# Row vectors by transfer, weights on GpSimd, and shared copies in a four-layer graph attention kernel on one Trainium2 core

## The reference

```python
# layer 0: 4 heads of 32
scores = where(adj == 0, -inf, q @ k.T / sqrt(32));  out = softmax(scores) @ v;  out @ wo.T + bo
# layer 1 (one head), layer 2 (8 heads of 16, plus beta*log(adj + 1e-6)), layer 3 (two GATs with MLPs between)
e = leaky_relu(s1[:, None] + s2[None, :], 0.2);  attention = softmax(masked e);  out = attention @ h
# layer 3: relu(x W + b) -> GAT over all pairs, 256 wide -> elu(elu) + residual -> relu(x W + b)
#          -> GAT over adj, 128 wide -> elu(elu) + residual -> relu
```

## Time and profile before

| | us |
|---|---|
| median of 3 runs | 1078.31 |
| lowest, highest | 1078.24, 1078.61 |
| the profiled execution | 1080.22 |
| its span, first to last instruction | 1078.4 |

### The profile page before, as it was taken

One profiled execution on the slowest core, in us unless ns is written; L12 is line 12 of the kernel. 1 busy time (PEld: TensorE's weight loads), 2 busy tenths in 40 slices (PEclk: granted clock), 3 DMA queues, 4 the chain that ended last, 5 costly groups with the idle time before them and its releaser, 6 DMA issues. The chain is left out here.

```text
span 1078.4 us, 26660 instructions
## 1 busy us (share of the span) xinstructions
PE 1024.1 (95%) x9189; PEld 760.1 (70%) x9189; DVE 914.3 (85%) x2533; ACT 771.2 (72%) x2029; POOL 272.7 (25%) x606
## 2 busy tenths in 40 slices
PE   7989999999999999999999999999999999899985
PEld 5667767667677777868577776777676777666784
DVE  4656999998999988999899799989899798988543
ACT  3979858775777788768886977868867875544543
POOL 1012414131323224222212332223213232220101
PEclk9999999999999999999999999999999999999998
DMA  4000212202020200202030031112020021020000
GB/s 127 2 11 12 90 29 63 70 21 76 16 78 14 90 11 21 80 22 79 2 100 11 12 90 56 35 33 69 21 80 2 25 67 60 30 72 19 11 11 20
DMA packets 30468, 46.81 MB, mean 43 GB/s; under 512 B 6912, under 2 KB 9216, under 8 KB 30336
## 3 DMA queue, kind: packets, MB, share of 16 engines
q1 hardware_dynamic: 29472, 44.84, 13.4%
q10 hardware_dynamic: 864, 0.26, 0.1%
HBM read 40.64 MB, written 4.46 MB: 42 GB/s over the span
## 5 line engine op out<-in xcount | busy, mean ns | idle before, releaser
L1230 DVE SCALAR_TENSOR_TENSOR P<-row,t2e,mask_t 128x512 f32<-128x512 f32 x512 | 355.9, 755 | 11.2 <-PE bank L608 10.4
L766 ACT ACTIVATE probs<-probs,neg_max 128x512 f32<-128x512 f32 x256 | 186.7, 732 | 35.6 <-DVE neg_max L1046 35.6
L1038 DVE CUSTOM_DVE_ANT_0 probs<-bank,mask_add 128x512 f32<-128x512 f32 x256 | 169.5, 677 | 20.4 <-PE bank L503 19.8
L776 ACT ACTIVATE probs_t<-bank 128x512 f32<-128x512 f32 x256 | 151.0, 610 | 12.7 <-PE bank L511 12.2
L511 PE MATMUL bank<-ident,probs 128*128 128x128 f32 x1024 | 142.7, 277 | 5.1 <-ACT probs L766 3.1
L511 PEld LDWEIGHTS bank<-ident,probs 128*128 128x128 f32 x1024 | 114.0, 141 | 37.5 <-ACT probs L766 19.9
L811 ACT ACTIVATE x<-x,shift_l,rstd_l 128x128 f32<-128x128 f32 x256 | 105.3, 487 | 38.9 <-POOL shift_l L1368 38.9
L608 PE MATMUL bank<-P,GH 128*32 128x512 f32 x1024 | 116.4, 595 | 4.5 <-issue 3.2
L653 PE MATMUL bank<-t,l_P 128*128 128x258 f32 x512 | 119.8, 383 | 1.0 <-DVE l_P L1152 0.9
L1353 POOL TENSOR_TENSOR rstd_l<-mv_l,ln_eps 128x4 f32<-128x4 f32 x64 | 16.1, 252 | 384.0 <-DVE mv_l L1092 383.8
L653 PEld LDWEIGHTS bank<-t,l_P 128*128 128x128 f32 x512 | 93.8, 190 | 16.7 <-issue 2.5
(11 more groups left out here) (168 smaller groups left out, 1922.5 us busy)
## 6 DMA issues: line engine op xcount, KB each, us to landing
row<-line SPq DMA_DIRECT2D x128, 256.0 KB, 3.7
x_in<-in_x SPq DMA_DIRECT2D x16, 256.0 KB, 2.8
out<-x SPq DMA_DIRECT2D x16, 256.0 KB, 2.0
l_P<-in_adj SPq DMA_DIRECT2D x4, 256.0 KB, 5.2
w_fc<-in_L_gnn_W_fc SPq DMA_DIRECT2D x1, 256.0 KB, 4.2
P<-in_L_gnn_a_fc SPq DMA_DIRECT2D x1, 256.0 KB, 3.5
line<-turned SPq DMA_DIRECT2D x16, 16.0 KB
w_cat<-in_L_gnn_W SPq DMA_DIRECT2D x2, 64.0 KB, 4.1
```

The costliest lines, as they stand in the source:

```text
L766: act.activation(e, e, ACT.Exp, bias=neg_max[:, m:m + 1], scale=SCALE0, accum_out=g.of(den0)[:, m:m + 1])\
L776: act.activation(probs_t[c % 2][:, h, :, :].rearrange("p j n -> p (j n)"), ps("l0_t", g, m)[:, :], ACT.Copy)\
L1038: dve.tensor_tensor_reduce(probs[c % 2][:, h, :], ps("l0_s", g, m)[:, :], mask_add[:, c, :], 1.0, -3.0e38, ALU.add, ALU.max, row_max[:, m: ...
L1230: last = dve.scalar_tensor_tensor(P2[:, h % GROUP2, j, :], row(g, h)[:, :], g.of(t2e)[:, j, h:h + 1], mask_t[:, j, :], ALU.max, ALU.mult)
```

## The change

In graphs 2 to 11 (`ROWS_BY_DMA`) the rows of layers 0, 1 and 3 take the way of layer 2's: VectorE turns a block (`turn`), SyncE writes a line and reads it to all partitions, and TensorE's `l0_rd`, `l1_s`, `l3_s` and `l3b_s` are left out. In those graphs GpSimd, not VectorE, makes layer 3's first weights (`l3_p`) and layer 0's product (`l0_o`), from the row buffer. There are six row buffers, handed out by a table. In graphs 0 to 2 (`SPLIT_TURNED`) VectorE copies every second turned tile (24 in all). The maximum of layer 0's scores becomes a minimum of negated scores, so that `l0_neg` goes for all graphs and an exponential waits for its own tile only. In graphs 12 to 15 (`IN_HALVES`) the end of layer 3 works on chunk pairs, and `l3_r` no longer waits for `l3b_z`; layernorm's four instructions signal each, and the last store is in two parts. All order tables are written anew; the stage `warm` stands in them 65 times in place of 90.

```diff
-MASKED = -1.0e30
+MASKED, LOWEST = 1.0e30, 1.0e20
...
-ROWS = 5
+ROWS = 6
...
+IN_HALVES = range(12, 16)
+SPLIT_TURNED = range(0, 3)
+ROWS_BY_DMA = range(2, 12)
...
-    "sp": "0:adj_load 1:late_loads 3:out_load a:x_load f:l2_rows g:l2_spread l:store",
+    "sp": "0:adj_load 1:late_loads 3:out_load a:x_load b:l0_rows c:l0_spread d:l1_rows e:l1_spread "
+          "f:l2_rows g:l2_spread h:l3_rows i:l3_spread j:l3b_rows k:l3b_spread l:store",
...
+def row_uses():
+
+    used, transfers, last, at = {}, [0] * ROWS, [None] * ROWS, 0
+    for name, g, k in turns("sp"):
+        if name.endswith("_spread"):
+            r = int(ROW_OF_USE[at])
+            at += 1
+            transfers[r] += 1
+            used[name, k, g.i] = r, transfers[r], last[r]
+            last[r] = name, k, g
+    return used
+
...
+        def part(g, k):
+
+            return (2 * k, 2 * k + 2, 1) if g.i in IN_HALVES else (0, C, 2)
...
+        def by_dma(g, back=0):
+            return g.i - back in ROWS_BY_DMA
+
+        def dma_sig(name, g, k=1, back=0):
+
+            return signal[name], per_graph[name] * ROWS_BY_DMA.index(g.i - back) + k
+
+        def sources_read(n, g, back=0):
+
+            return dma_sig(n + "_p", g, 1, back) if by_dma(g, back) else took(n + "_s", g, 0, back)
+
+        def divided(g, back=0):
+
+            return dma_sig("o0_made", g, 1, back) if by_dma(g, back) else took("l0_rd", g, 0, back)
+
...
+        def row(stage, g, k=0):
+            return rows[row_use[stage, k, g.i][0]]
+
+        def spread_done(stage, g, k=0):
+
+            r, transfers, _ = row_use[stage, k, g.i]
+            return row_filled[r], 16 * transfers
...
+        def row_read(stage, g, k):
+
+            if stage == "l2_spread":
+                return sig("p2_made", g, k + 1)
+            return divided(g) if stage == "l0_spread" else sources_read(stage[:-len("_spread")], g)
...
+            def lay_out(n, turned):
+                def f(g, k):
+                    sp.wait_ge(*(sig if n == "l2" else dma_sig)(n + "_turned", g, 1))
+                    if n == "l0" and by_dma(g, 2):
+                        sp.wait_ge(*divided(g, back=2))
+                    sp.dma_start(g.of(line[n]).rearrange("r (q s) -> q r s", s=BLOCK),
+                                 turned[:, :]).then_inc(signal[n + "_rows"], 16)
+                return f
+
+            def free_row(stage, g, k):
+                r, _, last = row_use[stage, k, g.i]
+                if last:
+                    sp.wait_ge(*row_read(last[0], last[2], last[1]))
+                return rows[r], row_filled[r]
+
+            def spread(n):
+                def f(g, k):
+                    if k == 0:
+                        sp.wait_ge(*(sig if n == "l2" else dma_sig)(n + "_rows", g, 16))
+                    to, done = free_row(n + "_spread", g, k)
+                    sp.dma_start(to[:, :], g.of(line[n])[k * C:(k + 1) * C, :].rearrange("c p -> (c p)")
+                                 .rearrange("(o n) -> o n", o=1).broadcast_to([P, N_NODES])).then_inc(done, 16)
+                return f
+
+            def l0_spread(g, k):
+                sp.wait_ge(*dma_sig("l0_rows", g, 16))
+                to, done = free_row("l0_spread", g, k)
+                sp.dma_start(to[:, :],
+                             g.of(line["l0"])[0:HEADS0 * C, :].rearrange("(h c) p -> h (c p)", h=HEADS0).unsqueeze(1)
...
-                pe.wait_ge(*took("l0_rd", g))
+                pe.wait_ge(*divided(g))
...
-                        pe.wait_ge(*took(n + "_s", g))
+                        pe.wait_ge(*sources_read(n, g))
...
-                    pe.wait_ge(*took("l3_s", g))
+                    pe.wait_ge(*sources_read("l3", g))
...
             def l3_r(g, k):
-                pe.wait_ge(*sig("z4_made", g, 1))
+                if g.i in IN_HALVES:
+                    pe.wait_ge(*took("l3_m2", g))
+                else:
+                    pe.wait_ge(*sig("z4_made", g, 2))
...
-                if m % HEADS0 == 0:
-                    act.wait_ge(*sig("neg_max0", g, m // HEADS0 + 1))
+                act.wait_ge(*took("l0_s", g, m))
...
                 e = probs[m // HEADS0 % 2][:, m % HEADS0, :]
-                act.activation(e, e, ACT.Exp, bias=neg_max[:, m:m + 1], scale=SCALE0, accum_out=g.of(den0)[:, m:m + 1])\
+                act.activation(e, e, ACT.Exp, bias=low0[:, m:m + 1], scale=-1.0, accum_out=g.of(den0)[:, m:m + 1])\
                     .then_inc(signal["exp0"], 1)
...
-            def l0_t(g, m):
+            def l0_t(g, k):
+                m = 2 * k if g.i in SPLIT_TURNED else k
                 c, h = m // HEADS0, m % HEADS0
...
-                dve.tensor_tensor_reduce(probs[c % 2][:, h, :], ps("l0_s", g, m)[:, :], mask_add[:, c, :], 1.0, -3.0e38,
-                                         ALU.add, ALU.max, row_max[:, m:m + 1]).then_inc(emptied("l0_s", g, m), 1)
-
-            def l0_neg(g, c):
-                dve.wait_ge(*took("l0_s", g, HEADS0 * c + HEADS0 - 1))
-                if g.has(1):
-                    dve.wait_ge(*sig("exp0", g, HEADS0 * c + HEADS0, back=1))
-                q = slice(HEADS0 * c, HEADS0 * (c + 1))
-                dve.tensor_scalar(neg_max[:, q], row_max[:, q], -1.0e20, -SCALE0, ALU.max, ALU.mult)\
-                    .then_inc(signal["neg_max0"], 1)
+                dve.tensor_tensor_reduce(probs[c % 2][:, h, :], ps("l0_s", g, m)[:, :], mask_add[:, c, :], 1.0, LOWEST,
+                                         ALU.add, ALU.min, low0[:, m:m + 1]).then_inc(emptied("l0_s", g, m), 1)
+
+            def l0_t(g, k):
+                m = 2 * k + 1
+                c, h = m // HEADS0, m % HEADS0
+                dve.wait_ge(*wrote("l0_t", g, m))
+                if h == 1 and c >= 2:
+                    dve.wait_ge(*wrote("l0_pv", g, c - 2))
+                elif h == 1 and g.has(1):
+                    dve.wait_ge(*wrote("l0_pv", g, c + 2, back=1))
+                dve.tensor_copy(probs_t[c % 2][:, h, :, :].rearrange("p j n -> p (j n)"), ps("l0_t", g, m)[:, :])\
+                    .then_inc(emptied("l0_t", g, m), 1)
...
+            def turn(n, column, made, turned):
+
+                def f(g, k):
+                    dve.wait_ge(*made(g))
+                    if n == "l2" and g.has(1):
+                        dve.wait_ge(*sig("l2_rows", g, 16, back=1))
+                    elif n != "l2" and by_dma(g, 1):
+                        dve.wait_ge(*dma_sig(n + "_rows", g, 16, back=1))
+                    dve.transpose(turned[:, :], column(g)).then_inc(signal[n + "_turned"], 1)
...
+            def sources(n, g):
+                return row(n + "_spread", g)[:, :] if by_dma(g) else ps(n + "_s", g)[:, :]
...
+                        made.then_inc(signal[n + "_p"] if by_dma(g) else emptied(n + "_s", g), 1)
...
             def l3_z(g, k):
-                dve.wait_ge(*sig("l3_eb", g, 1))
-                dve.scalar_tensor_tensor(v3[:, :, :], e3[:, :, :], -1.0, v3[:, :, :], ALU.add, ALU.max)\
-                    .then_inc(signal["z3_made"], 1)
+                c0, c1, made = part(g, k)
+                dve.wait_ge(*sig("l3_eb", g, k + made))
+                dve.scalar_tensor_tensor(v3[:, c0:c1, :], e3[:, c0:c1, :], -1.0, v3[:, c0:c1, :], ALU.add, ALU.max)\
+                    .then_inc(signal["z3_made"], made)
...
+            def l0_o(g, k):
+                pool.wait_ge(*spread_done("l0_spread", g))
+                for c in range(C):
+                    pool.wait_ge(*took("l0_pv", g, c))
+                pool.wait_ge(*wrote("l0_y", g, back=1))
+                pool.tensor_tensor(o0_t[:, :], row("l0_spread", g)[:, :], o0_raw[:, :], ALU.mult).then_inc(signal["o0_made"], 1)
+
+            def l3_p(g, j):
+                q = gat["l3"]
+                if j == 0:
+                    pool.wait_ge(*sig("l3_b", g, 3))
+                    pool.wait_ge(*spread_done("l3_spread", g))
+                    pool.wait_ge(*wrote("l3_o", g, C - 1, back=1))
+                made = pool.tensor_scalar(q["P"][:, j, :], row("l3_spread", g)[:, :], q["g"][:, j:j + 1], q["b"][:, j:j + 1],
+                                          ALU.mult, ALU.max)
+                if j == C - 1:
+                    made.then_inc(signal["l3_p"], 1)
+
```

The tables change in every line. One line of TensorE's before and after, cut:

```diff
-        "n0i1n0f2f2f2f2e2g2f2f2f2f2a3j1g2b3k1c3g2k1o0d3l1e3p0p0m1f2f2f2f2q0e3r0g2h2f3f3f3i2f3n1e3f3n1f3f3f3j2"
+        "f2g2e2f2f2j1f2g2k1k1f2a3o0g2f2p0p0f2l1b3q0c3r0f2m1e3f2d3g2f3f3e3f3n1f3e3f3i2f3f3g3f3n1e3f3f3f3g3a4f3"
```

More of the change, by code:

```diff
@@ L317, in build_program @@
         for n in LAYERS:
-            for what, k in (("stats", 1), ("mv", 1), ("var", 2), ("rstd", 1), ("shift", 1), ("x", 1)):
+            for what, k in (("stats", 1), ("mv", 1), ("var", 2), ("rstd", 1), ("shift", 1), ("x", C)):
                 sem(f"{n}_{what}", k)
         for n in GATS:
-            for what, k in (("c4", 1), ("dd", 2), ("b", 3)):
+            for what, k in (("c4", 1), ("dd", 2), ("b", 3), ("turned", 1), ("p", 1)):
                 sem(f"{n}_{what}", k)
@@ L781, in l0_ov @@
```

(4 more changed lines are left out.)

427 lines of the change are left out of this document (224 added, 203 removed), and 8 rows, old and new, of the table STAGES.

## The result

The changed kernel takes 1067.03 us (median of 4 runs, 1064.78 to 1069.56) beside 1078.46 of the kernel before (4 runs on the same chip, 1078.24 to 1079.78): ratio 0.9892, 95% interval [0.9873, 0.9911]. It is faster by 11.4 us. The profiled execution took 1069.56 us, its span is 1067.7.

A forecast was written before the change was run, and what follows sets the result against it. TensorE, 98% busy from 110 to 869 us with VectorE (92%) close behind, was taken as the bound. 1080.2 - 29.4 (TensorE work) - 3 (start) - 5 (end) + 4 (waits, contention) = 1046.8, median 1.9 lower: 1045 us; range 1028 to 1066.

The forecast's parts named there:

- the first term: Graphs 2 to 11: row turns (18.8 us) and `l0_rd` (10.6) leave TensorE, taking 29.4 us off the time.
- The first rival: Half the gain is lost since TensorE's busy time is not its bound; dense 23 us go, 1059 us, chance 0.17.
- the one for the bound: Whole kernel: if TensorE's busy time falls and the time does not, the sum is wrong at the bound.
- one for the waits: Row waits over 15 us, `l3_o` waits over 10, or GpSimd weights over 2 us each: sum wrong there.
- Waits for rows: Graphs 2 to 11: VectorE waits 6.7 us more for rows by DMA; about half, 3.5 us, reaches the end.
- The second rival: SyncE's in-order queue holds new rows behind layer 2's waiting for a buffer; slower, 1085 us, chance 0.10.
- GpSimd: Graphs 2 to 11: 40 weights at 1.0 us and 10 products at 1.24; 325 us busy in all, no bound.
- VectorE 910.9 and not 891: Whole kernel: VectorE ends 23 us lighter, its busy time falling from 914.3 to near 891 us.
- TensorE 999.2 and not 982: Whole kernel: TensorE's busy time near 982 us, from 1024.1 less 29.4 and 100 fewer `warm` records.
- Start and end: Start, split copies in first graphs: 3 us gained (0 to 9); end, halves in last graphs: 5 (0 to 10).
- VectorE's relief: Middle, 110 to 869 us: VectorE 37 us lighter, no gain of its own but letting TensorE's come through.

The follow-up runs named there:

- the half-size weights: Changed kernel with GpSimd making only 256 of 512 columns of each fourth-layer weight in graphs 2 to 11: 1062.27 us, ratio 0.9858.
- small edits: Changed code with the old order, TensorE spreading rows, no halves or split copies; minimum, own-tile exponentials and chunks released singly remain: 1076.41 us, ratio 0.9983.
- The run with both cuts: Kernel before, graphs 2 to 11, with less TensorE spreading and VectorE's fourth-layer weights over 256 of 512 columns: 1074.95 us, ratio 0.9967.

## Why the prediction was wrong

**The step that failed is the first term, -29.4 us for work that leaves TensorE.** It took a stretch in which TensorE is busy for 98% as one in which a microsecond less of work is a microsecond less of time. Taken away by itself, 15.6 us of busy time gave 0.3 us (the interval goes from 2.3 us less to 0.9 more); 16.9 added cost 16.8. The 98% said truly that there was no room for more. It said nothing of what becomes of less. TensorE, VectorE and ScalarE pass each graph back and forth in fixed orders, and the traces of the cut kernels show most of each cut as idle time on the engine that was cut. The first rival came nearest, with its 1059 and its chance of 0.17, but its sum still let 23 of the 29.4 us through, so it fails at the same term: in the order of the kernel before next to nothing came through. Both signs that the prediction named have come, the one for the bound (TensorE's busy time falls and the time does not) and one for the waits (weights on GpSimd over 2 us each); the half-size weights tell them apart, with 4.8 us at most for the second. The Trainium skill (Perfetto Trace Analysis, Identifying the Most-Contended Engine) would optimize the engine of highest occupancy first, and judges TensorE by its share of peak FLOPs and by its weight loads. Loads at 70% did warn of slack that matmul busy time hides; but VectorE, at 92% the highest by that rule, gave 7.5 us for 44 as well. In these runs no share of busy time told what a cut would bring.

**What then gained 11.4 us?** The set of edits together with the order laid out for it, as far as the runs tell. In the new order undoing any part costs much: 6.6 (copies), 8.7 (halves), 8.9 (TensorE's work back), 11.1 (weights back); by the ratios, each to its own group's "before", 7.2, 9.7, 10.7 and 12.3. In the old order adding the parts gives 2.0 (small edits), 1.5 (halves) and -7.5 (hand-placed copies). The four undoings add up to 35 us, three times the whole gain, so they are no shares of it. Three of them also put work onto an engine whose order was not laid out for it, at places chosen by hand, and work added to TensorE cost time in the old order too; so they don't show what leaving the work out gained. That the new order by itself carries the gain was only argued: it can't run without the parts whose entries it holds, and it wasn't tried. How the 11.4 divide stays open.

**The other terms.**
- Waits for rows: small, as forecast. VectorE waited 3.0 us for rows in all (6.7 forecast), GpSimd's products 9.3. The second rival (SyncE's queue, 1085) did not come.
- GpSimd: wrong by a factor of two. I had no row of its tensor_scalar and took 1.0 us between 0.72 and 1.24; it is 2.07 at the median, 2.28 in the mean. The bound came from an instruction with two tensor inputs and one operation, and for that kind it was good: the products of 512 columns took 1.27 us at the median (1.24 forecast). A weight has two operations with a column each. That it would cost nothing "as long as `l3_o` is not waiting" held in the changed kernel (3 waits), with an eighth of its excess at most as the price.
- VectorE 910.9 and not 891: the layer 2 weights took 11.5 us more, the 80 weights from a row some 3 more than from a bank (the prediction has 60 of them; in ten graphs with two layers of four they are 80). I had counted 2.5 us for the contention of the first. The rest of the gap is spread over other groups.
- TensorE 999.2 and not 982: 100 `warm` records fewer gave 9.8, as forecast nearly (12.7), and the groups that leave gave 29.5. But 14 us came back in other groups: the 192 turns of `x` (L470, now L549) are 35.4 us busy and were 29.9, with the mean of one at 287 ns and not 278. In the emptier queue more sets stand alone and bring a start-up of their own.
- Start and end: 3 (0 to 9) and 5 (0 to 10) forecast. Undoing the copies cost 6.6 and undoing the halves 8.7, of which the traces place 5.0 behind graph 15's layer 2. As separate gains both are inside their bounds, but they are not separate.
- The other side of the same mistake: I argued that VectorE's relief (37 us in the middle) "lets TensorE's come through". The run with both cuts gave 3 us.

## What to carry to other kernels

Where several engines run hand-ordered queues, a busy share near 100% prices added work, not removed work: price a removal by what waits for that very instruction, or by a run with the work cut and nothing else. Expect little from a cut in an order that was laid out with the work in it, and before calling a part the cause try it both ways: added in the old order and undone in the new one. Before work goes to an engine for the first time, one such instruction in a trace is worth more than a slope from another kind.
